# Taking one of GpSimd's waits out of the first layer of a two-layer graph network

## What is computed

```
h = relu(layernorm(x))
# first layer, one row per edge
m = concat(h[src], edge_attr) @ W1 + b1
m = silu(layernorm(m) * g1 + be1)
m = silu(m @ W2 + b2)
agg = segment_sum(m, dst)
x = x + layernorm(silu(concat(agg, h) @ Wu + bu)) * gn + bn
# second layer
h = relu(layernorm(x))
agg = segment_sum(h[src], dst)
x = x + relu((h + agg) @ M1 + c1) @ M2 + c2
```

## Time and profile before

| | us |
|---|---|
| time, median of 3 runs | 6198.23 |
| lowest and highest of them | 6190.43 and 6201.92 |
| span of the profiled execution, first to last instruction | 6194.4 |
| GpSimd busy | 4331.5 (70% of the span) |
| TensorE busy | 3949.3 (64%) |
| VectorE busy | 2502.4 (40%) |
| ScalarE busy | 2070.8 (33%) |

### The profile page before, as it was taken

The page is one execution under the profiler, slowest core; times in us unless marked ns, Lnnn a source line. Parts: engine busy times, 40 slices in busy tenths (PEclk is TensorE's granted clock), DMA queues, the critical chain, the costliest instruction groups (busy, mean ns, idle before and its releaser), DMA issues. The chain is left out here.

```text
span 6194.4 us, 75337 instructions
## 1 busy us (share of the span) xinstructions
PE 3949.3 (64%) x23603; PEld 3229.6 (52%) x23603; DVE 2502.4 (40%) x5222; ACT 2070.8 (33%) x2908; POOL 4331.5 (70%) x4165
## 2 busy tenths in 40 slices
PE   6455555555555555555555555555576999999999
PEld 5234344444444444444444434444455888888886
DVE  6322222222232222222222222222376777777751
ACT  2022222222222222222222222222235777777751
POOL 3777777777777777777777777777656777777861
PEclk9566767677676667776766676676658999999995
DMA  3111111111111111111111111111121000000011
GB/s 93 44 36 35 37 36 36 37 36 37 37 36 36 36 37 37 36 36 37 36 37 37 36 36 36 37 37 36 27 51 25 22 22 22 22 22 22 22 25 33
DMA packets 256727, 216.83 MB, mean 35 GB/s; under 512 B 138460, under 2 KB 188953, under 8 KB 256007
## 3 DMA queue, kind: packets, MB, share of 16 engines
q0 software_dynamic: 133248, 136.74, 10.2%
q1 hardware_dynamic: 123271, 77.59, 4.3%
HBM read 199.53 MB, written 14.40 MB: 35 GB/s over the span
## 5 line engine op out<-in xcount | busy, mean ns | idle before, releaser
L719 POOL DMA_INDIRECT gat<-layer_rows,idx x3992 | 4115.7, 1031 | 1477.5 <-issue 1057.8
L764 PE MATMUL ps<-one_hots,edge_buffers 128*128 128x80 f32 x3128 | 687.5, 392 | 1890.9 <-DVE cT L808 1890.9
L764 PEld LDWEIGHTS ps<-one_hots,edge_buffers 128*128 128x128 f32 x3128 | 621.3, 295 | 2243.3 <-issue 2243.3
L1015 DVE TENSOR_TENSOR edge_buffers<-ps,gat 128x512 f32<-128x512 f32 x391 | 270.2, 691 | 2948.1 <-DMA gat<-layer_rows,idx 2390.0
L1574 ACT ACTIVATE node_buffers<-ps 125x800 bf16<-125x800 f32 x1152 | 954.2, 839 | 342.3 <-PE ps L1625 278.8
L970 ACT ACTIVATE edge_buffers<-ps,gcol 128x512 f32<-128x512 f32 x391 | 302.6, 774 | 2142.9 <-PE ps L739 2142.8
L732 PE MATMUL ps<-w1e,edge_buffers 128*128 128x256 f32 x1564 | 739.6, 625 | 114.7 <-DVE edge_buffers L1015 110.7
L1604 PE MATMUL ps<-edge_buffers,node_buffers 125*128 125x192 bf16 x7200 | 764.8, 247 | 0.0
L1604 PEld LDWEIGHTS ps<-edge_buffers,node_buffers 125*128 125x128 bf16 x7200 | 666.4, 140 | 12.3 <-issue 12.2
L1625 PE MATMUL ps<-node_buffers 128*128 128x200 bf16 x4608 | 607.3, 255 | 59.8 <-ACT node_buffers L1574 45.6
L1683 DVE TENSOR_TENSOR node_buffers<-ioh,node_buffers 128x1600 bf16<-128x1600 bf16 x576 | 567.3, 985 | 0.0
(11 more groups left out here) (182 smaller groups left out, 3075.4 us busy)
## 6 DMA issues: line engine op xcount, KB each, us to landing
gat<-layer_rows,idx POOLq DMA_INDIRECT x3992
edge_buffers<-in_edge_quads SPq DMA_DIRECT2D x391, 128.0 KB, 2.1
node_buffers<-in_x SPq DMA_DIRECT2D x5, 625.0 KB
layer_rows<-node_buffers SPq DMA_DIRECT2D x25, 125.0 KB
residual_rows<-node_buffers SPq DMA_DIRECT2D x5, 625.0 KB
layer_rows<-node_buffers SPq DMA_DIRECT2D x5, 625.0 KB
node_buffers<-residual_rows POOLq DMA_DIRECT2D x25, 125.0 KB, 4.4
out<-node_buffers SPq DMA_DIRECT2D x25, 125.0 KB
```

The lines of the kernel that those rows point to most:

```text
L719: pool.indirect_dma_start(out=gat[:, j, c, :], out_offset=None, in_=table[:, :], in_offset=bass.IndirectOffsetOnAxis(ap=idx[:, half, j, c: ...
L764: mm = pe.matmul(to[:, 0:2 * WIN], rows_of[:, 2 * k:2 * k + 2, :].rearrange("p c f -> p (c f)"), oh[:, j, 2 * k:2 * k + 2, :].rearrange("p ...
```

## The change

GpSimd's wait for landed rows behind every third block is taken out. The other waits, the transfers, their order and the buffers are as before.

```diff
                         wait(pool, g_z, n - AHEAD + 1)
                         wait_alone(pool, "gpsimd")
                         gather(pool, ptab, j // UN, s, g_gat[s])
-                        if n % 3 == 2 and n + 1 < BLOCKS:
-
-                            wait(pool, g_gat[s], rows_before(e, j) * (16 * BC) + 16 * BC)
                 with pool.If(flagged(pool) == 0):
                     rounds(step, 0)
```

## The result

The changed kernel takes 5929.3 us (median of 4 runs, 5915.9 to 5934.5), the kernel before beside it 6200.1 us (6190.4 to 6205.5). The ratio is 0.956, with a 95% interval of 0.9545 to 0.9574. So 271 us are gone, 18 us more than the 252 forecast; 5946 us were forecast, 5912 to 5980 as the range.

A forecast was written before the change was run, and what follows sets the result against it. GpSimd's issue of the first layer's transfers was taken as the bound. Removing pauses (247.7 us) and longer first transfers behind them (4 us) was taken as 252.2 us off 6198.2 us: 5946 us, range 5912 to 5980.

The forecast's parts named there:

- What bounds the stage: First layer's transfers, 4270.4 us: GpSimd issues as fast as it can except at 130 places; the others wait for it.
- What the change removes, 247.7 us: First layer: 130 pauses sum to 286.7 us; ordinary pauses of 39.0 us remain, so 247.7 us go.
- What it moves, 4 us: First layer: shifted overlap of transfers with VectorE's instructions; 4 us for longer first transfers behind pauses.
- blocks that already run the way all will run: First-layer blocks with n % 3 = 1, no wait before or behind: four give 10.28 us each, the price for all 391.
- 34 us to either side: First-layer spread: one transfer lengthened beside VectorE more or fewer per four blocks, 34 us, so 5912 to 5980 us.
- the 4019: Forecast length in us of the first layer's transfer stage: 391 blocks at 10.28 us, against 4270.4 before.
- What could be late next: First layer: the other engines and GpSimd's remaining waits keep up with a block every 10.28 us instead of 10.92.
- cover of 31 us: GpSimd's wait before block n for the addition of block n-4: three blocks, 31 us, lie between, so no pause.
- Piling up: Rival: without pauses the first layer's transfer queue backs up and issue slows, 6651 us; chance 3 in 100.
- More meetings: Rival: more first-layer transfers lengthened beside VectorE; 114 us gained, 6084 us, or no gain at all; chance 6 in 100.
- Fewer meetings: Rival: all first-layer blocks run like the remainder-2 one, 9.99 us; 364 us gained, 5834 us; chance 3 in 100.
- Another wait: Rival: a wait for a place in `gat` or for indices replaces the removed one; no change, 6198 us; chance 2 in 100.

The follow-up runs named there:

- the kernel with 33 waits: The kernel before with its wait only behind every twelfth block (n % 12 == 2), 33 waits instead of 130: 5966.5 us, ratio 0.9642.
- the changed kernel's second profile: The changed kernel run again, unedited, as a base on another chip: 5918.5 us, ratio 0.9558.
- the two kernels with 33 waits: The kernel before with waits only at n % 12 == 2 (5966.5 us, 0.9642) or, one block later, at n % 12 == 3 (5993.0 us, 0.9687).
- AHEAD = 2: The changed kernel with GpSimd held to two blocks ahead of VectorE's additions instead of four: 5914.3 us.
- short scaling: The changed kernel with VectorE's scaling done for one of a block's eight columns, from the fifth block on: 5859.1 us, ratio 0.94.

## Why the prediction was right, point by point

**What bounds the stage:** right. GpSimd issues without a break, the 0.3 us between transfers are all that is left of its idle time, and every kernel's time on the ordinary chips followed GpSimd's idle and busy time.

**What the change removes, 247.7 us:** right. The 130 long pauses are gone and none took their place. With the wait put back for rows already there, the gain stayed whole. The count holds for the profiled execution, in which rows landed sooner than in all others on the ordinary chips. With pauses of 2.28 us, as in the kernel with 33 waits, it would be 257 us (an estimate), of the 270 gained on the second chip.

**What it moves, 4 us:** the right mechanism at the wrong size; this is the step that failed. The term was 36 us in the profiled pair (3070.3 to 3034.4 us busy), and 247.7 + 36.0 = 283.7 against 283.1 measured in the stage. With the changed kernel's second profile it was 26 us. What failed is the price by "blocks that already run the way all will run". The four blocks weren't a bad draw: over the whole trace, blocks with n % 3 = 1 take 10.28 us as an average of the four remainders. But in the changed kernel a block takes 3987.3 / 391 = 10.20 us, and 10.22 in the second profile. The 36 us have two halves.

One half, 18 us, is in the 131 blocks that stand first or behind a pause. Of the 130 first transfers there 95 were long, 42 us in all; in the changed kernel the first transfers have 0.4 us. Against that the pause took meetings away later in the same block, most at remainder 3. The prediction had the 1.39 us in its rows, but took four blocks without a pause before them and called the 4 us between its two counts the price of the long first transfer. Moving the wait by one block, with as many pauses, changed GpSimd's busy time by 26 us, so this half is shown. (In the row at 2032.05 the scaling L1038 was running when the transfer began, not L771: it had 0.57 us left, and 0.57 - 0.12 = 0.45 = 1.39 - 0.94.)

The other half, also 18 us, is in the blocks with no pause before them. Those with n % 3 = 1 have 0.24 to 0.26 us of extra length at remainders 0 and 1 and 0.14 at remainder 2 in the kernel before; the changed kernel's two profiles have 0.12 to 0.19 and at most 0.04 there. It would be natural to say that a pause still acts on the block after next, but the two kernels with 33 waits speak against it: there that block has 0.14 and 0.15. What does differ is the landing, 0.06 us sooner in the profile of the kernel before, and VectorE's work follows the landing. At remainders 0 and 1 its one-hots began 0.10 us before the block's third transfer (median), in the changed kernel 0.04 us before it, and the boundary found above is 0.03 us. About nine in ten of these third transfers were long in the kernel before, and five or six in ten in the changed kernel. That the sooner landing made these meetings is argued from these numbers; no run changed the landing alone, so the cause of this half stays open.

So the time came into the range because the range had 34 us to either side, which the error of this term nearly used up: the stage was 32 us below the 4019. One of the prediction's own signs failed by it: GpSimd's busy time was to be within 15 us of 3070. Transfers above 1 us became fewer, 278 after 364.

**What could be late next:** right on the chips like the first. The granted clock in the stage rose from 0.69 to 0.71 and no chain of waits took over. It is wrong as a general statement: on the third chip the cover of 31 us at the wait for block n-4 was used up, by TensorE's stops.

**The rivals.** Piling up fell: the mean length grew by 0.004 us in a run of 3,128 and the landing not at all, nothing grew with 96 between pauses, and the depth had no effect. More meetings fell; there were fewer. Fewer meetings is what happened, by far less than the rival had (it took the best kind for all blocks, 112 us beyond the forecast; the runs gave 18). Another wait took no place.

## What to carry to other kernels

When one engine's queue is the bound, a wait in it for something that it doesn't itself need costs the whole idle time, and that can be counted in one profile: 247.7 of the 271 us here. What such a count leaves out is how the engine's own instructions meet with those of the others. Here that turned on hundredths of a microsecond: it was worth 10 us between two executions of one kernel and 26 us between two places for 33 waits. So sum it over the whole stage rather than over a few blocks, read a second execution before calling a difference the change's, and give it a spread of some 30 us. Blocks that happen to have no wait near them aren't proof of how a kernel without waits will run.

Long VectorE instructions with two inputs in SBUF are worth moving away from the starts of GpSimd's transfers: one swap of two lines in VectorE's order gave 37 us more (5881.9 us, the fastest kernel here that computes all). With no meeting at all it would be 85 to 95 us, by the two profiles of the changed kernel.

## What wasn't expected of the hardware

With a wait behind every block, GpSimd had a pause of 1.4 us in the middle of a block's transfers, released by nothing in the profile, 32 times, each 96 transfers behind the one before, some 149 us. One row of its timeline:

```profile
964.55 0.94 POOL L719 DMA_INDIRECT gat<-layer_rows,idx  x1 [1.41 <-issue]
```

No other kernel here had a series of them, and their cause is open. Two of the eight executions of the kernels with `AHEAD = 2` and with short scaling were 80 us faster than their fellows, at a mean granted clock of 0.783 and 0.788 where the others had 0.772 to 0.777. They weren't profiled, so where that time came from is open too.
